# Four-layer network on one core: choice on logits, count in two parts, row numbers from GpSimd, gates in a second pass

## The reference

```python
x = input_emb.reshape(G, T, H)                      # G = 2 groups of T = 2048 tokens
router_probs = softmax(x @ w_router)                # 8 experts
gate, idx = top_k(router_probs, 2)
mask = one_hot(idx, 8)
mask_kt = swapaxes(mask, 1, 2).reshape(G, 2 * T, 8) # all first choices, then all second ones
pos = cumsum(mask_kt, 1) * mask_kt - 1              # place in the expert's queue, capacity 160
expert_out = relu(expert_in @ wi) @ wo              # expert_in: the chosen rows, in places
y = sum over choices of gate * expert_out[place]
```

## Time and profile before

| what | us |
|---|---|
| median of three runs | 901.35 |
| the profiled execution | 900.24 |
| its span, first to last instruction | 898.6 |
| busy: TensorE, VectorE, ScalarE, GpSimd | 822.4, 601.6, 484.7, 269.1 |

### The profile page before, as it was taken

The page is one execution under the profiler, slowest core; times in us unless marked ns, Lnnn a source line. Parts: engine busy times, 40 slices in busy tenths (PEclk is TensorE's granted clock), DMA queues, the critical chain, the costliest instruction groups (busy, mean ns, idle before and its releaser), DMA issues. The chain is left out here.

```text
span 898.6 us, 23310 instructions
## 1 busy us (share of the span) xinstructions
PE 822.4 (92%) x8906; PEld 670.6 (75%) x8906; DVE 601.6 (67%) x1403; ACT 484.7 (54%) x1008; POOL 269.1 (30%) x333
## 2 busy tenths in 40 slices
PE   6999999999899999998999899998899779999960
PEld 5888888887577777766777688886555549999950
DVE  3677778777557777777655335676667876757627
ACT  2544444443777777766964245654664315455425
POOL 1266663221202222223000000224452042656344
PEclk9999999999999999999999999999999789999985
DMA  8500000000000000002477444443222213566439
GB/s 320 193 25 18 18 23 18 20 9 3 1 1 1 1 2 1 1 1 71 125 195 182 108 128 116 127 147 135 95 94 94 94 36 112 140 193 166 122 63 341
DMA packets 74637, 79.55 MB, mean 89 GB/s; under 512 B 21824, under 2 KB 65728, under 8 KB 74176
## 3 DMA queue, kind: packets, MB, share of 16 engines
q1 hardware_dynamic: 69584, 72.36, 26.2%
q0 software_dynamic: 3968, 5.25, 3.4%
q10 hardware_dynamic: 1008, 0.91, 0.3%
HBM read 50.70 MB, written 27.79 MB: 87 GB/s over the span
## 5 line engine op out<-in xcount | busy, mean ns | idle before, releaser
L727 DVE TENSOR_TENSOR r_prob<-r_pS,const 128x512 f32<-128x512 f32 x128 | 81.9, 681 | 24.7 <-PE r_pS L549 24.7
L1104 DVE SCALAR_TENSOR_TENSOR f_gl<-att_res,small_first,f_gh 128x512 fp32r<-128x512 f32 x64 | 47.3, 747 | 35.8 <-ACT f_gh L1029 33.5
L958 PE MATMUL f_pY<-wpjT,f_gh 128*128 128x256 f32 x256 | 65.4, 290 | 0.3 <-DVE f_gl L1104 0.3
L1671 POOL TENSOR_TENSOR att_res<-att_res,t_hy 128x1024 f32<-128x1024 f32 x8 | 15.5, 1960 | 165.0 <-DVEq L2141 165.0
L959 PE MATMUL f_pY<-wpjT,f_gl 128*128 128x256 f32 x256 | 62.7, 279 | 0.0
L1372 PEld LDWEIGHTS q_bank<-q_xT,att_res 128*64 128x64 f32 x1024 | 57.3, 140 | 7.2 <-issue 4.2
L2507 POOL DMA_INDIRECT sum_dram<-e_yo,y_id x24 | 43.1, 1795 | 60.1 <-ACT e_yo L2641 45.0
L1372 PE MATMUL q_bank<-q_xT,att_res 128*64 128x128 f32 x1024 | 60.9, 279 | 0.0
L958 PEld LDWEIGHTS f_pY<-wpjT,f_gh 128*128 128x128 f32 x256 | 48.1, 188 | 15.9 <-issue 13.4
L1023 ACT ACTIVATE att_res<-f_pH 128x512 f32<-128x512 f32 x64 | 38.0, 594 | 38.6 <-PE f_pH L943 37.8
L2622 ACT ACTIVATE e_hh<-e_pH 128x320 fp32r<-128x320 f32 x64 | 26.2, 433 | 53.7 <-PE e_pH L2546 53.4
(11 more groups left out here) (321 smaller groups left out, 2354.5 us busy)
## 6 DMA issues: line engine op xcount, KB each, us to landing
kv_dram<-att_res SPq DMA_DIRECT2D x32, 256.0 KB, 3.4
t_ring<-kv_dram SPq DMA_DIRECT2D x128, 64.0 KB, 2.3
wi<-L_ffn_wi SPq DMA_DIRECT2D x8, 1024.0 KB, 5.0
wo<-L_ffn_wo SPq DMA_DIRECT2D x8, 1024.0 KB, 7.8
x_res<-L_attn_x SPq DMA_DIRECT2D x8, 512.0 KB, 6.9
q_dram<-att_res SPq DMA_DIRECT2D x16, 256.0 KB, 3.4
t_q<-q_dram SPq DMA_DIRECT2D x8, 512.0 KB, 4.1
x_dram<-x_res SPq DMA_DIRECT2D x8, 512.0 KB, 3.0
```

What stands on the lines that cost most here:

```text
L727: dve.tensor_tensor(prob[t % 2][:, r, :, :], pS[r][:, :, :], dec[:, r, :, :], ALU.mult)\
L958: pe.matmul(out, gh[c % 4][:, cols], net.wpjT[:, c, :], start=(c == 0 and t % 2 == 0), stop=False, skip_group_check=True)
L1104: dve.scalar_tensor_tensor(out=gl[c % 4][:, :], in0=g[c][:, :], scalar=net.lnw[:, c:c + 1], in1=gh[c % 4][:, :], op0=ALU.mult, op1=ALU.sub ...
```

## The change

For group 1 the choice is made on the logits (`choose_last`): only the top logit is taken, both picks follow, and the softmax's exponential is fed by a subtraction on GpSimd. The mask is signalled in two halves, and `count` starts on the first choice's half. GpSimd multiplies the mask of group 1 by the token's words (`give_sources`); the gates of group 1 are computed and given only after the row numbers for fetching (`gates_of_last`, `give_gates`), and TensorE's product of group 1 is made in two passes, words 0 to 2 and then the gate's words. `one_hot` compares bf16 slot numbers with one place at a time (8 instructions of 128x160 for one of 128x1280), and ScalarE makes the fourth part for both groups. `place(1)` stands directly behind the choice. The raw sums are copied at the end (`keep_words`) into the room of the logits, and `y_id` and `slot_gate` are made of them in the experts' phase (`ways_back`, behind expert 0's split; ScalarE and GpSimd wait for it). Two of the four quarters of `low_part` and the fetches of parts 1 and 2 of expert 1 move to the experts' phase too. Fillers: 2, 4 and 2 are new, 14, 14 and 20 become 3, 5 and 10.

```diff
@@ -172,6 +172,8 @@
...
+        own_and_spare = 2 * WORDS * EXPERTS
+        self.words = self.lg[:, :, :].rearrange("p t e -> p (t e)")[:, 0:MGROUPS * own_and_spare].rearrange("p (g s w) -> p g s w", g=MGROUPS, s=2)
@@ -1575,8 +1577,10 @@
...
+    numbers = mp.sb("numbers", [P, CAP], BF16)
+    OF_ACT = 8
...
-    idf, apart = mp.sb("idf", [P, 2, 2, EXPERTS]), mp.sb("apart", [P, 8, CAP])
+    idf, apart = mp.sb("idf", [P, 2, 2, EXPERTS]), mp.sb("apart", [P, OF_ACT + 1, CAP])
@@ -1622,6 +1626,16 @@
...
+    def give_sources(eng, g):
...
+        what = sources[:, g * PAIRS * 3:(g + 1) * PAIRS * 3].rearrange("p (n v a) -> p n v a", v=3, a=1)
+        eng.wait_ge(mask_ready.sem, mask_ready.after(2 * g + 1))
+        ins = eng.tensor_tensor(given[:, g, :, 0:3, :], mask_of_all(g), what.broadcast_to([P, PAIRS, 3, EXPERTS]), ALU.mult)
+        if g:
+            ins.then_inc(given_ready.sem, 1)
@@ -1705,14 +1719,17 @@
...
+        pool.wait_ge(shifted.sem, shifted.after(2))
+        tops = m1[:, TPG:].rearrange("p (t a) -> p t a", a=1).broadcast_to([P, TPG, EXPERTS])
+        pool.tensor_tensor(pr[:, TPG:, :], lg[:, TPG:, :], tops, ALU.subtract).then_inc(shifted.sem, 1)
+        give_sources(pool, 1)
...
         pool.wait_ge(x_id_ready.sem, x_id_ready.after(1))
         for e in two:
             fetch_rows(net, pool, e, 0)
         pool.wait_ge(x_id_ready.sem, x_id_ready.after(2))
-        for e in two:
-            for r in (1, 2):
-                fetch_rows(net, pool, e, r)
+        for r in (1, 2):
+            fetch_rows(net, pool, 0, r)
@@ -1845,29 +1862,37 @@
...
-            pe.wait_ge(mask_ready.sem, mask_ready.after(g + 1))
...
-            pe.matmul(pC, tri[:, :], chosen.rearrange("p n e -> p (n e)"), start=True, stop=False, skip_group_check=True)
-            for n in range(PAIRS - 1):
-                behind = PAIRS - 1 - n
-                mm = pe.matmul(pC[:, (n + 1) * EXPERTS:], ones[:, :], chosen[:, n:n + 1, :].broadcast_to([P, behind, EXPERTS]),
...
+            for k in range(TOPK):
+                pe.wait_ge(mask_ready.sem, mask_ready.after(g + 1 + g * k))
+                mine = slice(k * TPG, (k + 1) * TPG)
+                mm = pe.matmul(pC[:, k * TPG * EXPERTS:(k + 1) * TPG * EXPERTS], tri[:, :], chosen[:, mine, :].rearrange("p n e -> p (n e)"),
+                               start=(k == 0), stop=(k == TOPK - 1), skip_group_check=True)
+                for n in range(PAIRS - 1)[mine]:
+                    behind = PAIRS - 1 - n
+                    mm = pe.matmul(pC[:, (n + 1) * EXPERTS:], ones[:, :], chosen[:, n:n + 1, :].broadcast_to([P, behind, EXPERTS]),
+                                   start=False, stop=(behind == 1), skip_group_check=True)
...
-        def ids(g):
+        def ids(g, words, stage):
...
-            pe.wait_ge(given_ready.sem, given_ready.after(g + 1))
+            pe.wait_ge(given_ready.sem, given_ready.after(stage))
+            if stage == 3:
+                pe.wait_ge(x_id_ready.sem, x_id_ready.after(2))
+            first, width = words.start * EXPERTS, (words.stop - words.start) * EXPERTS
...
-                if n == PAIRS - 8 and g:
-                    pe.wait_ge(tables_ready.sem, tables_ready.after(3))
+                if n == PAIRS - OF_ACT:
+                    pe.wait_ge(tables_ready.sem, tables_ready.after(4 + g))
                 elif n % 8 == 0:
-                    pe.wait_ge(hot_ready.sem, hot_ready.after(4 * g + n // 8 + 1))
-                what = given[:, g, n, :, :].rearrange("p v e -> p (v e)")
...
+                    pe.wait_ge(hot_ready.sem, hot_ready.after(3 * g + n // 8 + 1))
+                what = given[:, g, n, words, :].rearrange("p v e -> p (v e)")
+                pe.matmul(pI[g][:, first:first + width], hot[:, n, 0:P], what,
+                          start=(n == 0 and first == 0), stop=(n == PAIRS - 1), skip_group_check=True)
+                mm = pe.matmul(pI[g][:, WORDS * EXPERTS + first:WORDS * EXPERTS + first + width], hot[:, n, SPARE:CAP], what,
@@ -1890,6 +1915,7 @@
...
                 count(0, BATCH - 2)
+                keep_turning(pe, pH[1], ones[:, :], 2)
                 logits(b - 1)
@@ -1918,16 +1944,19 @@
...
+        keep_turning(pe, pH[1], ones[:, :], 4)
         turn_x(BATCH - 1, 0)
         turn_x(BATCH - 1, 1)
+        keep_turning(pe, pH[1], ones[:, :], 2)
         logits(BATCH - 1)
         turn_logits(BATCH - 1)
-        ids(0)
-        keep_turning(pe, pH[1], ones[:, :], 14)
+        ids(0, slice(0, WORDS), 1)
+        keep_turning(pe, pH[1], ones[:, :], 3)
         count(1, BATCH)
-        keep_turning(pe, pH[1], ones[:, :], 14)
-        ids(1)
-        keep_turning(pe, pH[1], ones[:, :], 20)
+        keep_turning(pe, pH[1], ones[:, :], 5)
+        ids(1, slice(0, 3), 2)
+        keep_turning(pe, pH[1], ones[:, :], 10)
+        ids(1, slice(3, WORDS), 3)
@@ -2006,8 +2035,21 @@
...
-            act.wait_ge(shifted.sem, shifted.after(g + 1))
-            nc.scalar.activation(pr[:, tiles, :], lg[:, tiles, :], ACT.Exp).then_inc(exped.sem, 1)
+            act.wait_ge(shifted.sem, shifted.after(2 * g + 1))
+            nc.scalar.activation(pr[:, tiles, :], (pr if g else lg)[:, tiles, :], ACT.Exp).then_inc(exped.sem, 1)
+
+        def distances(g):
+            act.wait_ge(p_taken.sem, p_taken.after(2 * g + 2))
+            for n in range(PAIRS - OF_ACT, PAIRS):
+                ins = nc.scalar.activation(apart[:, n - PAIRS + OF_ACT + 1, :], slots, ACT.Square, bias=posk[:, g, n:n + 1], scale=-1.0)
+            ins.then_inc(row_squared.sem, 1)
+
+        def near(g):
+            act.wait_ge(row_squared.sem, row_squared.after(TILES + 1 + g))
+            if g:
+                act.wait_ge(ids_made.sem, ids_made.after(g))
+            nc.scalar.activation(hot[:, PAIRS - OF_ACT:PAIRS, :], apart[:, 1:OF_ACT + 1, :], ACT.Relu, bias=net.table["ones"][:, 0:1], scale=-1.0)\
+                .then_inc(tables_ready.sem, 1)
@@ -2043,6 +2085,8 @@
...
                 exp(0)
+                act.wait_ge(route_in.sem, route_in.after(16))
+                nc.scalar.activation(numbers[:, :], slots, ACT.Copy).then_inc(tables_ready.sem, 1)
@@ -2064,7 +2108,9 @@
...
         keep_turned_logits(BATCH - 2)
+        distances(0)
         take_x(BATCH - 1, 0)
+        near(0)
         keep_turned_logits(BATCH - 1)
         exp(1)
@@ -2073,13 +2119,8 @@
...
+        distances(1)
+        near(1)
@@ -2249,12 +2290,54 @@
...
-        def give(g):
...
-            dve.wait_ge(mask_ready.sem, mask_ready.after(g + 1))
-            dve.tensor_tensor(given[:, g, :, 0:3, :], chosen, what.broadcast_to([P, PAIRS, 3, EXPERTS]), ALU.mult)
+        def choose_last():
...
+            def lowest(of, best, chosen):
+                dve.tensor_tensor(ranks, of, each(best), ALU.is_equal).then_inc(steps.sem, 1)
+                dve.wait_ge(steps.sem, steps.done(1))
+                dve.tensor_tensor(ranks, ranks, first, ALU.mult).then_inc(steps.sem, 1)
...
+                dve.tensor_reduce(rank, ranks, AX.X, ALU.max).then_inc(steps.sem, 1)
...
+                dve.tensor_tensor(chosen, ranks, each(rank), ALU.is_equal).then_inc(steps.sem, 1)
...
+            dve.wait_ge(l_taken.sem, l_taken.after(BATCH))
+            dve.tensor_reduce(top, lgg, AX.X, ALU.max).then_inc(shifted.sem, 1)
+            dve.wait_ge(shifted.sem, shifted.after(2))
+            lowest(lgg, top, mask[:, 1, 0, :, :])
+            dve.sem_inc(mask_ready.sem, 1)
+            dve.scalar_tensor_tensor(out=least, in0=mask[:, 1, 0, :, :], scalar=-3.0e38, in1=lgg, op0=ALU.mult, op1=ALU.add).then_inc(steps.sem, 1)
+            dve.wait_ge(steps.sem, steps.done(1))
+            dve.tensor_reduce(second, least, AX.X, ALU.max).then_inc(steps.sem, 1)
+            dve.wait_ge(steps.sem, steps.done(1))
+            lowest(least, second, mask[:, 1, 1, :, :])
+            dve.sem_inc(mask_ready.sem, 1)
...
+        def gates_of_last():
...
+            dve.wait_ge(exped.sem, exped.after(2))
+            dve.scalar_tensor_tensor(out=s8[:, tiles, :], in0=mask[:, 1, 0, :, :], scalar=-2.0, in1=prg, op0=ALU.mult, op1=ALU.add)
+            dve.tensor_reduce(total, prg, AX.X, ALU.add).then_inc(steps.sem, 1)
...
+            dve.reciprocal(net.gates[:, 0, tiles], total)
+            dve.tensor_reduce(m1[:, tiles], s8[:, tiles, :], AX.X, ALU.max).then_inc(steps.sem, 1)
...
+            dve.tensor_tensor(net.gates[:, 1, tiles], m1[:, tiles], net.gates[:, 0, tiles], ALU.mult).then_inc(steps.sem, 1)
...
+        def give_gates(g):
@@ -2267,70 +2350,61 @@
...
+            dve.tensor_tensor(given[:, g, :, 3:6, :], mask_of_all(g), each, ALU.mult).then_inc(given_ready.sem, 1)
...
         def place(g):
...
-            dve.wait_ge(p_taken.sem, p_taken.after(g + 1))
-            ins = dve.tensor_reduce(posk[:, g, :], pos[:, :, :], AX.X, ALU.add).then_inc(steps.sem, 1)
-            dve.wait_ge(steps.sem, steps.done(1))
-            if g:
-                dve.sem_inc(p_taken.sem, 1)
```

(59 more changed lines are left out.)

74 lines of the change are left out of this document (39 added, 35 removed).

## The result

The changed kernel took 891.77 us in the median of four runs (890.56 to 893.27), beside 901.14 us (898.96 to 901.55) for the kernel before: a ratio of 0.989, interval 0.9864 to 0.9916. The profiled execution took 892.54 us, its span is 890.9 us; before it was 900.24 and 898.6.

A forecast was written before the change was run, and what follows sets the result against it. VectorE's order of work was taken to bound the stretch before the experts, TensorE the rest. Terms -7.1 -0.3 +0.35 +0.2 +0.2 gave -6.6 us, subtracted from the 901.35 us median: 894.8 us, range 892.8 to 899.0.

The forecast's parts named there:

- The seam goes by VectorE's order: From 706.82 to 730.70 us VectorE has hardly a gap and its order of work sets when expert 0's transposes start.
- The price of a one-hot instruction: VectorE's 128x160 bf16 comparison costs 0.169 us, 1.35 us a part, equal to the old one; the rewriting itself wins nothing.
- Rivals 2 to 5: One-hot instruction price: f32 rate 0.210 us (15%), one element a step 0.294 (6%), no overlap 0.378 (4%), cheap 0.102 (7%).
- VectorE's stretch: First one-hot part to reading group 1's ids: 16.8 us against 23.9, so 7.1 us earlier.
- From the read to the transposes: Reading group 1's ids to expert 0's transposes: 6.3 us against 6.56, 0.3 earlier, TensorE arriving last.
- The experts' start: Two low-part quarters of wi ahead of VectorE's front outlast the transposes: +0.35 us; the ways back there are free.
- Given back elsewhere: Losses beyond the experts' start: up to +0.2 us in the batches, +0.2 us for VectorE and GpSimd working at once.
- +0.2 us in the batches: ScalarE's copy of the numbers (0.3) stands ahead of a copy TensorE wants: up to +0.2 us.
- +0.2 us for VectorE beside GpSimd: VectorE and GpSimd working at once costs 0 to +0.4 us, taken as +0.2.
- rival 5: Cheap one-hot instructions: 48 at 0.102 us, -3.2 us, 891.6 us; 7%.
- Clock rival: TensorE drops to 1.2 GHz near 707 us despite new fillers, pushing the count's second part 1.7 us: 896.5 us; 12%.
- The same price: TensorE's clock falls at the experts' start, half of a low stretch, 1.7 us, is lost: 896.5 us; 5%.

The follow-up runs named there:

- second trace of the kernel after: The changed kernel run again with nothing changed: 893.98 us beside 902.05 us for the kernel before, ratio 0.9925.
- second trace of the kernel before: The kernel before run again unchanged, against itself: 900.7 us beside 902.05 us for its own runs, ratio 0.999.
- later pairs of medians: The changed kernel, unchanged, timed twice more against the kernel before: 893.98 beside 902.05 us and 894.41 beside 902.45 us.

## Why the prediction was right in its mechanism and short in its size

**The seam goes by VectorE's order, and the experts' rounds are untouched: right.** All but 0.4 us of the 7.7 lie in the seam.

**The price of a one-hot instruction: right.** 16 of them, from 708.43 to the copy at 711.17 us, are 0.171 us apart; forecast 0.169. Three parts of eight cost 1.46 and 2.87 us where 1.35 and 2.78 stood in the sum. Rivals 2 to 5 (0.210, 0.294, 0.378 and 0.102 us) are out. The Trainium skill (VectorE: DVE Perf Modes, The perf-mode tier table) gives four elements a cycle for this form; an estimate by it, with the 0.127 us of the earlier trace rows, is 0.169 us, and the trace agrees. By the 58 cycles fixed that the Trainium skill gives (VectorE: DVE Perf Modes, The TRN2 errata) the estimate is 0.102 us, and the trace is 0.069 us above it.

**VectorE's stretch: right term by term but the last.** One-hot and copy to the logits' copy 4.70 us (forecast 4.65); copy, choice and the wait for the count 4.81 (711.17 to 715.98; forecast 0.22 + 3.70 + 0.85 = 4.77); place 0.91 (1.03); first part with group 0's row numbers 1.91 (2.00); the last two parts to the read 4.00 (2.78 + 1.56 = 4.34). Sum 16.33, forecast 16.79. The last term failed: the wait behind the last part is 1.13 us where 1.56 was carried over whole from the earlier trace rows. The pass now multiplies 24 columns instead of 48, for which the sum took nothing off. That is where the time went: from the first to the last of the 32 products behind the last hot part it is 0.85 us (0.027 apart), before 1.25 us (0.040 apart), both at 1.2 GHz; from the last one's start to the read it is 0.22 us, before 0.25. In the second trace of the kernel after the 0.85 us are the same, but the wait is 1.46 us by what lies behind the last product. So the first trace has 0.34 us in its favour that this same code doesn't always have.

**From the read to the transposes: 6.52 us, forecast 6.3.** Direct: 0.3 us earlier than before was expected, 0.04 came. VectorE, with 723.58 to 728.94 us of gates, low parts and copies, arrives last at the phase's end, 0.27 us behind TensorE, where the text had TensorE. The path is the forecast one all the same: VectorE's last copy (728.68 us) waits 0.48 us for TensorE's last product of the gate words. The undone ways back show that this end has no slack.

**The experts' start: right.** Front behind the low quarters: the transposes to the first product take 3.16 us (before 2.84), +0.32 for a forecast of +0.35. The ways back end at 733.96 us, and the first low part, at 734.25 us, has waited 0.29 us for ScalarE and not for them. Free, as costed.

**Given back elsewhere: wrong, 0.4 us.** The +0.2 us in the batches and +0.2 us for VectorE beside GpSimd didn't show. The 0.35 us by which the first one-hot instruction is earlier can't be put down to the change either: in the other traces of the same code it stands later by up to 2.7 us; against such shifts 0.2 us in the batches could not be seen in any case. The sharing is real, but the fetch beside the one-hot tables got shorter, from 2.08 us to 1.60 us, and no fetch ends last in the kernel after.

**From the sum to the time: the steps that failed.** Two steps make up the 3.0 us between forecast and median. The smaller is the sum. The seam's own terms (-7.1, -0.3, +0.35, +0.2) gave -6.85 us, and it measures -7.27 on the first pair of traces. With the 0.2 of the batches and the 0.35 ahead of the seam, the sum of -6.6 us falls 1.1 us short of the 7.7 by which the spans differ. The term that was mis-sized is the wait behind the last hot part, 1.56 us for a measured 1.13, beside the 0.4 us given back that didn't show. The larger step, 1.9 us, is the one from the profiled execution to the median: the forecast took the profiled execution of before as 1.1 us below its median and carried that over, but the median after lies 0.77 us below its profiled execution. The later pairs of medians differ by 8.1 and 8.0 us. Against them the sum is short by 1.4 to 1.5 us. The range's lower end of 892.8 us lies 0.6 us below the 893.4 that the forecast has on its own terms, though the prediction itself says that a measurement of this kernel can tell 1.8 us. It left too little room for where a median of four runs falls, and it left out rival 5, the only one that points down. That the first median lies below the range and the two later ones (893.98 and 894.41 us) inside it is a matter of that scatter.

**Clock rival.** It didn't fall at 707 us: TensorE was busy 2.25 of the 3.0 us ahead of it and stayed at 2.4 GHz. That the new fillers held it is likely but not shown: in the second trace of the kernel before it didn't fall there either, without them. The price of 1.7 us was too high: the fall costs about 0.6 us of the seam where it comes. The same price for 3.4 us at 1.2 GHz at the experts' start was too high too: in seven traces that have such a stretch there the first round, from expert 0's transposes to expert 1's, takes 0.3 to 0.7 us more than in the same order without it.
